# Keeping the residual stream with tokens on the partitions in a six-layer local-attention kernel, shifting it by DMA and normalising it with batch statistics

## What is computed

```python
def shift_tokens(t):              # features 64..127 come from the token before
    a, s = jnp.split(t, 2, -1)
    s = jnp.pad(s, ((0, 0), (1, 0), (0, 0)))[:, :-1]
    return jnp.concatenate([a, s], -1)
...
for i in range(DEPTH):
    x = attn_layer(shift_tokens(x), Wqkv[i], q_scale[i], k_scale[i], Wo[i]) + x
    x = ffn_layer(shift_tokens(x), ln_g[i], ln_b[i], W1[i], b1[i], W2[i], b2[i]) + x
```

## Time and profile before

| | |
|---|---|
| median of 3 runs | 3686.34 us |
| profiled execution, span from first to last instruction | 3699.1 us |
| TensorE matmul busy | 3521.4 us (95%), 63940 instructions |
| TensorE weight load busy | 2694.0 us (73%) |
| VectorE busy | 3039.5 us (82%) |
| ScalarE busy | 2586.6 us (70%) |
| GpSimd busy | 2309.1 us (62%) |
| mean granted TensorE clock | 0.987 |
| `part_a`, `part_b`, `part_c` | to about 588 us, to about 3679 us, to the end |

### The profile page before, as it was taken

The page is one execution under the profiler, slowest core; times in us unless marked ns, Lnnn a source line. Parts: engine busy times, 40 slices in busy tenths (PEclk is TensorE's granted clock), DMA queues, the critical chain, the costliest instruction groups (busy, mean ns, idle before and its releaser), DMA issues. The chain is left out here.

```text
span 3699.1 us, 146879 instructions
## 1 busy us (share of the span) xinstructions
PE 3521.4 (95%) x63940; PEld 2694.0 (73%) x63940; DVE 3039.5 (82%) x4947; ACT 2586.6 (70%) x4028; POOL 2309.1 (62%) x1364
## 2 busy tenths in 40 slices
PE   6999996999999999999999999999999999999996
PEld 4777774777777777777777777777777777777774
DVE  5767766988889988888888888888898888888883
ACT  3565554677777777777777777777777777777773
POOL 1110104767777777777777767777777777776761
PEclk9999998999999999999999999999999999999998
DMA  2000001212222222222222222222222222222212
GB/s 75 4 4 7 4 7 43 56 48 58 56 58 63 64 56 58 56 56 62 58 56 58 54 56 64 56 58 55 64 63 58 56 57 54 56 56 54 54 49 68
DMA packets 121989, 188.76 MB, mean 51 GB/s; under 512 B 24942, under 2 KB 43142, under 8 KB 120972
## 3 DMA queue, kind: packets, MB, share of 16 engines
q1 hardware_dynamic: 121356, 179.36, 18.7%
HBM read 24.08 MB, written 4.19 MB: 8 GB/s over the span
## 5 line engine op out<-in xcount | busy, mean ns | idle before, releaser
L1325 POOL TENSOR_TENSOR rc<-rc,rs 128x1024 f32<-128x1024 f32 x384 | 912.9, 2377 | 349.2 <-DVE rs L1391 348.5
L1331 POOL TENSOR_TENSOR rc<-rc,rnorm 128x1024 f32<-128x1024 f32 x384 | 723.7, 1906 | 392.9 <-DVE rnorm L162 331.4
L1385 DVE TENSOR_TENSOR rc<-proj,rope_b 128x1024 f32<-128x1024 f32 x384 | 466.7, 1215 | 96.1 <-ACT squares L1177 89.6
L1177 ACT ACTIVATE squares<-proj 128x1024 f32<-128x1024 f32 x384 | 394.0, 1026 | 151.1 <-PE proj L921 137.6
L1013 PEld LDWEIGHTS ring<-pT,vmoved 64*64 64x64 f32 x18432 | 381.2, 135 | 132.8 <-issue 132.8
L1391 DVE TENSOR_TENSOR rs<-proj,rope_b 128x1024 f32<-128x1024 f32 x384 | 466.2, 1214 | 0.0
L958 PEld LDWEIGHTS ring<-ident,rc 128*128 128x128 f32 x3072 | 364.2, 142 | 137.5 <-issue 52.2
L1399 DVE TENSOR_REDUCE sums<-squares 128x16 f32<-128x1024 f32 x384 | 455.3, 1186 | 1.1 <-issue 0.9
L1013 PE MATMUL ring<-pT,vmoved 64*64 64x32 f32 x18432 | 407.7, 220 | 37.9 <-issue 36.4
L958 PE MATMUL ring<-ident,rc 128*128 128x128 f32 x3072 | 426.3, 277 | 11.6 <-POOL rc L1331 6.6
L1013 PE MATMUL ring<-pT,vown 64*64 64x32 f32 x6144 | 381.9, 219 | 13.8 <-issue 13.8
(11 more groups left out here) (176 smaller groups left out, 7886.1 us busy)
## 6 DMA issues: line engine op xcount, KB each, us to landing
vmoved<-vown SPq DMA_DIRECT2D x576, 128.0 KB
vmoved<-vown SPq DMA_DIRECT2D x192, 192.0 KB
vmoved<-vown SPq DMA_DIRECT2D x576, 64.0 KB
wqkv_raw<-in_L_ffn_Wqkv SPq DMA_DIRECT2D x40, 192.0 KB, 2.7
wo<-in_L_ffn_Wo SPq DMA_DIRECT2D x6, 512.0 KB, 4.2
x_attended<-xtok SPq DMA_DIRECT2D x8, 256.0 KB, 2.0
xtok_c<-x_attended SPq DMA_DIRECT2D x8, 256.0 KB, 4.2
out<-xtok_c SPq DMA_DIRECT2D x8, 256.0 KB, 2.4
```

Source lines behind the costliest of these rows:

```text
L1177: nc.scalar.activation(squares[:, c, :], proj[c][:, :], ACT.Square).then_inc(sq_done, 1)
L1325: nc.gpsimd.tensor_tensor(rc[:, k % 2, c, :], rc[:, k % 2, c, :], rs[:, c, :], ALU.add).then_inc(add_done, 1)
L1331: nc.gpsimd.tensor_tensor(dst, dst, rnorm[:, k % 2, c * HEADS:(c + 1) * HEADS].rearrange("p (h o) -> p h o", o=1).broadcast_to([P, HEADS, ...
L1385: nc.vector.tensor_tensor(rc[:, k % 2, c, :].rearrange("p (h d) -> p h d", h=HEADS), proj[c][:, :].rearrange("p (h d) -> p h d", h=HEADS), ...
```

## The change

The stream is kept as `xres`, 128 tokens of a tile on the partitions, 4 tiles by 128 features along the free axis. In `part_b`:

- The token shift is made by DMA from SBUF to SBUF: four transfers for each shift, one of the unshifted 64 features, three of the shifted ones, in pieces of 256 bytes. It is done once for the attention input (`move_in`) and once for the feed-forward input (`move_mid`), both in SyncE's queue behind the seven `vmoved` of a tile.
- The attention input is then transposed by TensorE (`turn_input`), copied from PSUM to `xa_hi` by ScalarE in one piece, and subtracted from the same PSUM bank into `xa_lo` by VectorE (`stage_lo`), which GpSimd did before in four pieces.
- `mean`, `variance`, `spread` and their ScalarE and VectorE steps are gone. VectorE takes `bn_stats` and `bn_aggr` of each tile (`moments`), ScalarE applies scale and shift by token (`apply_norm`, four activations of 128 x 128), TensorE transposes the four tiles (`turn_normed`).
- `output` and `feed_down` make token-major results: the activations are stationary and the weights move, 128 columns at a time.
- The second bias `b2` is a row of `w2` against a row of ones in `hid`.

`part_a` makes the second norm's output token-major (two multiplications with a row on GpSimd, instead of four transposes and a ScalarE evacuation), and `part_c` multiplies by a transposed gate row on VectorE and adds on GpSimd.

```diff
+            def shift_tokens(dst, n, sem):
+                half = DIM // 2
+                src = xres[:, (n % BATCH) * TILES:(n % BATCH + 1) * TILES, :]
+                sp.dma_start(dst[:, :, 0:half], src[:, :, 0:half]).then_inc(sem, 16)
+                sp.dma_start(dst[1:113, :, half:], src[0:112, :, half:]).then_inc(sem, 16)
+                sp.dma_start(dst[113:P, :, half:], src[112:P - 1, :, half:]).then_inc(sem, 16)
+                sp.dma_start(dst[0:1, 1:TILES, half:], src[P - 1:P, 0:TILES - 1, half:]).then_inc(sem, 16)
...
+                if j == 0 and n + 1 < NSEQ:
+                    move_in(n + 1)
+                if j == 1 and n:
+                    move_mid(n - 1)
                 if j == 1 and n + BATCH + 1 < NSEQ:
...
+            def turn_input(n, g):
+                pe.wait_ge(in_moved, 64 * (n + 1))
+                proj_emptied(0, g + 1)
+                for i in range(TILES):
+                    last = nc.tensor.transpose(proj_bank(0, 1)[:, i * P:(i + 1) * P], x_in[:, i, :], ident[:, :])
+                last.then_inc(in_full, 1)
...
-                for p in range(PAIRS):
-                    last = nc.tensor.matmul(bank[:, HALVES[half]], wo[:, p, :], oT[:, p, HALVES[half]],
-                                            start=(p == 0), stop=(p == PAIRS - 1))
+                for i in range(2):
+                    tok = slice((2 * half + i) * P, (2 * half + i + 1) * P)
+                    for p in range(PAIRS):
+                        last = nc.tensor.matmul(bank[:, i * P:(i + 1) * P], oT[:, p, tok], wo[:, p, :],
+                                                start=(p == 0), stop=(p == PAIRS - 1))
...
-                for i, (o, w) in enumerate(FFC):
-                    last = nc.tensor.matmul(bank[:, :], w2[0:w, i, :], hid[0:w, i, :], start=(i == 0), stop=(i == 2))
+                for j in range(TILES):
+                    tok = slice(j * P, (j + 1) * P)
+                    for i, w in enumerate((P, P, FF - 2 * P + 1)):
+                        last = nc.tensor.matmul(bank[:, tok], hid[0:w, i, tok], w2[0:w, i, :], start=(i == 0), stop=(i == 2))
...
-                if seq_at(g, 7) is not None:
-                    mean(seq_at(g, 7), g)
...
-                if seq_at(g, 7) is not None:
-                    variance(seq_at(g, 7), g)
...
                 if seq_at(g, 7) is not None:
-                    spread(seq_at(g, 7), g)
+                    turn_normed(seq_at(g, 7), g)
...
                 if seq_at(g, 10) is not None:
                     feed_down(seq_at(g, 10), g)
+                if seq_at(g, -2) is not None:
+                    turn_input(seq_at(g, -2), g)
...
+            def stage_input(n):
+                act.wait_ge(in_full, n + 1)
+                nc.scalar.activation(xa_hi[:, n % 2, :], proj_bank(0, 1), ACT.Copy).then_inc(x_hi_done, 1)
...
+            def apply_norm(n, k):
+                act.wait_ge(lead_done, n + 1)
+                act.wait_ge(mid_moved, 64 * (n + 1))
+                need(act, xn_full, n)
+                for i in range(TILES):
+                    nc.scalar.activation(xn[:, i, :], x_mid[:, i, :], ACT.Identity, bias=lead[:, i:i + 1],
+                                         scale=rnorm[:, k % 2, 2 * HEADS + i:2 * HEADS + i + 1]).then_inc(normed, 1)
...
+            def moments(n):
+                dve.wait_ge(mid_moved, 64 * (n + 1))
+                for i in range(TILES):
+                    nc.vector.bn_stats(stats[:, i:i + 1, :], x_mid[:, i:i + 1, :]).then_inc(stats_done, 1)
+                dve.wait_ge(stats_done, TILES * (n + 1))
+                need(dve, normed, TILES * n)
+                for i in range(TILES):
+                    nc.vector.bn_aggr(mv[:, i, :], stats[:, i, :]).then_inc(mv_done, 1)
+
+            def stage_lo(n):
+                dve.wait_ge(x_hi_done, n + 1)
+                nc.vector.tensor_tensor(xa_lo[:, n % 2, :], proj_bank(0, 1), xa_hi[:, n % 2, :].bitcast(f32),
+                                        ALU.subtract).then_inc(x_lo_done, 1)
...
-                if seq_at(g, 5) is not None:
-                    n = seq_at(g, 5)
-                    dve.wait_ge(mean_full, n + 1)
-                    need(dve, res_done, n)
-                    nc.vector.tensor_tensor(xc[:, :], xs[:, :], proj_bank(0, 0), ALU.subtract).then_inc(centred, 1)
                 if tile(g + 2):
                     square_sums(1, g + 2)
+                if seq_at(g, 5) is not None:
+                    moments(seq_at(g, 5))
+                if seq_at(g, -3) is not None:
+                    stage_lo(seq_at(g, -3))
```

More of the change, by code:

```diff
@@ L126, in program @@
         x_attended = nc.dram_tensor("x_attended", (P, BATCH * TILES, DIM), f32, kind="Internal").ap()
-        part_a(nc, t_in, alloc, need, x_attended, resT, ident, masks, mod, vecs, first_raw)
-        part_b(nc, t_in, alloc, need, resT, ident, win_mask, ident_bf, vecs, first_raw)
-        part_c(nc, out, alloc, need, x_attended, resT, ident, mod)
+        part_a(nc, t_in, alloc, need, x_attended, xres, ident, masks, mod, vecs, first_raw)
+        part_b(nc, t_in, alloc, need, xres, ident, win_mask, ident_bf, vecs, first_raw)
+        part_c(nc, out, alloc, need, x_attended, xres, ident, mod)
 CUBIC = math.sqrt(0.375)
@@ L842, in proj_bank, with tiles_of, by_tile @@
             return proj[c][:, k * 512:(k + 1) * 512]
+        def tiles_of(n, half):
+            first = (n % BATCH) * TILES + 2 * half
+            return xres[:, first:first + 2, :]
+        def by_tile(bank):
+            return bank.rearrange("p (t f) -> p t f", f=DIM)
         @block.sync
@@ L866, in load_chunk, with move_in, move_mid @@
                 sp.dma_start(w_raw[:, :], wqkv[layer, :, s * WCHUNK:(s + 1) * WCHUNK]).then_inc(raw_in, 16)
+            def shift_tokens(dst, n, sem):
[5 more added lines that the diff above has]
+                sp.dma_start(dst[0:1, 1:TILES, half:], src[P - 1:P, 0:TILES - 1, half:]).then_inc(sem, 16)
+            def move_in(n):
+                need(sp, in_full, n)
+                if n >= BATCH:
+                    sp.wait_ge(res_done, n - BATCH + 1)
+                shift_tokens(x_in, n, in_moved)
+            def move_mid(n):
+                sp.wait_ge(attn_added, 2 * n + 2)
+                need(sp, normed, TILES * n)
+                shift_tokens(x_mid, n, mid_moved)
+            sp.wait_ge(zeroed, 1)
+            move_in(0)
             load_qks(0)
@@ L872, in _ @@
             sp.wait_ge(w_lo_done, BATCH)
+            sp.wait_ge(ffn_ready, 2)
             load_chunk(BATCH)
-            for k in range(NT):
+            for k in range(NT + 2):
                 n, j = divmod(k, TILES)
+                if k >= NT:
+                    if j == 1:
+                        move_mid(n - 1)
+                    continue
                 sp.wait_ge(ring_free, RING["V1", k] + 1)
@@ L903, in _ @@
         def _(pe):
-            pe.wait_ge(zeroed, 6)
+            pe.wait_ge(zeroed, 3)
             def begin(name, k):
@@ L1107, in _ @@
                         pe.wait_ge(attn_added, 2 * seq_at(g, 6) + 2)
-                    if j == 3 and seq_at(g, 7) is not None:
-                        pe.wait_ge(var_read, seq_at(g, 7) + 1)
                     project(0, g + 1)
@@ L1223, in _ @@
                 if seq_at(g, 6) is not None:
-                    widen_deviation(g + 1)
-                if seq_at(g, -1) is not None:
-                    stage_hi(seq_at(g, -1), 1)
+                    apply_norm(seq_at(g, 6), g + 1)
                 if tile(g + 2):
@@ L1300, in load_vec @@
                 nc.gpsimd.tensor_copy(vec[:, :], vecs[:, :, layer]).then_inc(vec_done, 1)
-            def stage_lo(n, half):
-                count = 4 * n + 2 * half
-                for i, (rows, col, tok, width) in enumerate(stage[half]):
-                    pool.wait_ge(x_hi_done, count + i + 1)
-                    need(pool, x_lo_done, count + i)
-                    nc.gpsimd.tensor_tensor(xa_lo[rows, col:col + width], resT[rows, n % BATCH, tok:tok + width],
-                                            xa_hi[rows, col:col + width].bitcast(f32), ALU.subtract).then_inc(x_lo_done, 1)
-                pool.wait_ge(x_lo_done, count + 2)
             def make_rope(half, n):
@@ L1357, in _ @@
                     add_halves(1, t + 3)
-                if seq_at(t, -4) is not None:
-                    stage_lo(seq_at(t, -4), 0)
                 if tile(t + 3):
@@ L1367, in _ @@
                     make_rope(1, seq_at(t, -4))
-                if seq_at(t, -3) is not None:
-                    stage_lo(seq_at(t, -3), 1)
         @block.vector
         def _(dve):
-            dve.wait_ge(zeroed, 7)
+            dve.wait_ge(zeroed, 4)
             dve.wait_ge(consts_in, 16)
@@ L1448, in _ @@
                 late = seq_at(g, 8)
-                if seq_at(g, 7) is not None:
-                    dve.wait_ge(spread_full, seq_at(g, 7) + 1)
```

(1 more changed line is left out.)

197 lines of the change are left out of this document (92 added, 105 removed).

## The result

The changed kernel took 3747.55 us, the median of 4 runs (3741.43 to 3750.09), beside 3687.3 us for the kernel before on the same chip (4 runs, 3682.88 to 3696.49). The ratio is 1.0158, 95% interval 1.0141 to 1.0176. So it is slower by 1.6%, some 58 us, where the forecast was 3679 us and the range ended at 3722.

A forecast was written before the change was run, and what follows sets the result against it. TensorE's list was taken to set the pace, with VectorE's chain taking back nearly all its gain: delayed cycles win 20 us, quiet ones lose 12, so 8 us off 3686.3 gives 3679 us, range 3640 to 3722.

The forecast's parts named there:

- The short distances: Behind `norms_of`, results lead TensorE's need by 1.4 us at the second transposes and 1.2 us at `output`.
- the quiet cycle: A `part_b` cycle of 60.90 us in which TensorE never stands still; such cycles were forecast 0.6 us longer.
- The shift's landing at 8.64: `move_mid`'s shifted stream lands and VectorE's statistics start 8.64 us after the last `weigh`.
- rival 2: At `mid_moved` before `moments`, the shift lands late; at 2731.9 nearly all cycles lose, 3717 us; chance 0.20.
- a sign of being wrong: Quiet cycles of 59.7 us, VectorE's wait over 2 us, or granted clock under 0.97 in the middle.
- The delayed cycles: 26 of 44 full cycles have `output` more than 0.2 us late; each wins about 0.7 us.
- TensorE's list: TensorE's instructions per `part_b` cycle get 1.25 us shorter in sum; `mean` and `variance` go, `turn_input` and `output` add.
- GpSimd without `stage_lo`: GpSimd loses `stage_lo` in front of its scalings, but these wait for VectorE anyway: no gain.
- the four activations: ScalarE's four activations of 128 columns replacing `widen_deviation` take 1.5 us in all, against 0.6 for one wide copy.
- the 32 passes: `output` on TensorE becomes 32 passes of 128 columns, 0.11 us each, 3.55 us: +0.1, twice a cycle.
- the edges: The chain from L1271 to L1277 gets some 3 us shorter, `part_c` some 3 us longer: nothing together.
- VectorE's wait in 48 places: A sign of being right: VectorE idle before its first `bn_stats` on the DMA, about 1.3 us each.

The follow-up runs named there:

- Experiment 4: The kernel before, with four VectorE multiplications of 256 columns on a spare buffer added ahead of `norms_of`: 1.0123 of the kernel before.
- experiment 1: The changed kernel with the four shift DMAs into `x_mid` issued one step earlier: 1.0027 of the kernel before.
- Experiment 8: The changed kernel with the `x_mid` shift DMAs one step earlier and ScalarE's `stage_input` ahead of `values_out(g + 1, 0)`: 0.9908 of the kernel before.
- experiment 2: The changed kernel with VectorE's `stage_lo` ahead of `moments`: 1.0274 of the kernel before.

## Why the prediction was wrong, step by step

- **The short distances: this step failed.** I took 1.4 us of room at the second transposes and 1.2 us at `output`. The first transposes of the step, which start 1.0 us before the second ones in the quiet cycle, need a ring bank that the same evacuation frees, and had 0.2 us; `spread` had 0.1 us to VectorE's products. Experiment 4 shows it in the kernel before: 45 us for 1.55 us.
- **The shift's landing at 8.64: too early by 0.9 us.** On average over 42 cycles the first of the four was issued 5.0 us after the first `vmoved`, not 4.6, and the last one 2.5 us after that (2.41 in most cycles), not 1.95. The landing took 2.1 us from the last issue, where I took 2.0. It was 1.8 in the median and 2.3 to 3.2 in 12 cycles; why it was long in those stays open. So rival 2 came true, slower behind `mid_moved`, but in the main through the issues in the queue and not through the time that the small packets took to land. VectorE's wait of 2.5 us is over the 2 us that the prediction itself had named as a sign of being wrong. The rival's price, "nearly 1 us per cycle for each us", was right in this kernel: experiment 1 brought `norms_of` 1.0 us forward (medians) and won 1.0 us a cycle.
- **The delayed cycles: the sum had them win 0.7 us each, and they lost.** The quiet cycles came out near the forecast (0.9 us longer, predicted 0.6). But sorted by length, the middle cycle is 63.7 us instead of 63.0, and the one at three quarters 64.9 instead of 64.1. The whole 1.2 us of `output` in the delayed cycle could not be won, since a cycle that is late at `weigh` moves TensorE and the chain together, and the chain had become longer. That last reason is argued, not measured apart.
- **What waits behind the new wait.** I costed `stage_lo` as VectorE's time and not as a result that TensorE wants. `project(0)` waited for it in 24 cycles.
- **TensorE's list: -1.25 us, but not all of it could be used.** Its terms hold where rows show them (below, and `feed_down` with 2.68 us for its 24 passes, predicted 2.65); the whole was not measured apart. The second `mean` matmul hid ScalarE's mask copy; without it 0.34 us of the gain stops at the scores. Experiment 8 won 0.7 us a cycle.
- **GpSimd without `stage_lo`, "no gain": wrong in favour of the change.** It freed `norms_of`, which took 2.2 us instead of 3.4 (2764.59 to 2766.80 in the cycle above).
- **Near enough:** the four activations (1.65 us, predicted 1.5), the 32 passes (3.57 us from the first to what follows, predicted 3.55), the edges (nothing together), VectorE's wait in 48 places in kind, and no loss of clock in this kernel. The wait for GpSimd's second scaling did not come; TensorE waits for the evacuation ahead of it.

Together: the scores start 1.1 us later in a cycle than before, not later by 1.5, but the chain had 0.2 us of room at most and not 1.2. The gain of the shorter list was counted against the wrong place.

## What to carry to other kernels

Look for room at the **first** instruction that needs what a late engine frees, a PSUM bank as well as a result. Delay that chain by a known dose in the kernel before, and the price of being late there is measured before the change is made. A wait put into an in-order engine is paid by all that stands behind it, so a transfer whose source is ready a step earlier is issued a step earlier: here that alone was worth 48 of 58 us. Order the copies on a helping engine by who waits for them, not by where they are made.

## What the runs showed of the hardware

- The issue of a small transfer on SyncE's queue doesn't follow its size: 112 partitions of 1 KB in 256-byte pieces took 0.65 us, the 15 partitions behind them 0.94 us, and a single partition 0.75 us:

```profile
L893 SPq DMA_DIRECT2D first_raw<-xres x48: 652/652/666, 706.0 to 3697.5; - x48
...
L894 SPq DMA_DIRECT2D first_raw<-xres x48: 934/941/952, 706.7 to 3698.2; - x48
...
L895 SPq DMA_DIRECT2D first_raw<-xres x48: 746/753/761, 707.7 to 3699.2; - x48
```

- A VectorE instruction of 32 columns with its inputs in SBUF took up to 2.24 us beside a GpSimd addition, and 0.18 us without it. It ended 0.05 us after the addition did.
- Two waits of TensorE of about 1 us, some microseconds apart (0.97 and 1.08 in the cycle shown of the changed kernel), left the clock alone. In experiment 2, where the first of them was gone and the other longer, the passes behind it ran partly at 1.2 GHz in more than half of the cycles (24 of 42). In the one shown the waits were 1.85 and 0.45 us, and the granted clock was 0.76.
